# Layer 0's experts: rows fetched by a row list and answers scattered to a row per token and choice

## The chip, the cores and the metric

One core of a Trainium2 chip runs the whole program. The metric is the device time of one execution in microseconds (us), the median of several runs. The profile and the trace show one further execution.

The engines are named as in the profile: PE (TensorE matmuls) with PEld (its weight loads, which overlap the matmuls), DVE (VectorE), ACT (ScalarE), POOL (GpSimd) and SP (SyncE, which only issues transfers). Each runs its own list of instructions in order and waits on semaphores.

## The reference, cut to what matters

The model has four layers, each a cross attention and then a feed-forward part; 2 x 512 = 1024 tokens of 128 numbers. The change is in the feed-forward part of layer 0, whose end is a mixture of 16 experts with two choices per token. An expert takes at most 128 answers; of those that come in later, in token order, first choices first, none is computed:

```python
    B, S, D, H, E, F = (2, 128, 128, 16, 16, 512)     # B, S are taken from the input: 2 x 512
    xt = layer_norm(hidden, ln2_w, ln2_b).reshape(T, D)
    logits = xt @ router_w
    ...                                     # m1, m2: one-hot of the first and the second choice
    loc1 = jnp.cumsum(m1, axis=0) - 1.0
    loc2 = jnp.cumsum(m2, axis=0) - 1.0 + m1.sum(axis=0, keepdims=True)
    C = 2 * math.ceil(T / E)
    m1 = m1 * (loc1 < C)
    m2 = m2 * (loc2 < C)
    ...                                     # g1, g2: the two probabilities, normed to a sum of 1
    xin = jnp.einsum('tec,td->ecd', dispatch, xt)
    h = jnp.einsum('ecd,edf->ecf', xin, fc1_w) + fc1_b[:, None, :]
    h = jax.nn.gelu(h, approximate=False)
    eout = jnp.einsum('ecf,efd->ecd', h, fc2_w) + fc2_b[:, None, :]
    eout = eout * (1.0 - MOE_TOKEN_DROPOUT)
    moe_out = jnp.einsum('tec,ecd->td', combine, eout).reshape(b, s, D)
    return resid + moe_out
```

## The kernel before, in words

The four layers run one after the other. Tokens lie in SBUF as 8 tiles of 128 (`NT`); an expert's queue is one tile of 128 places. All arithmetic here is float32, in which each matmul shows as two rows of the trace.

**Places.** On DVE, `gating(0)` makes two one-hot masks (`top_mask`, L1786 to L1790; the last edit of the logits is L1808), the softmax (L1808 to L1812), and running sums of the masks (L1817 to L1820). PE turns these into the place of every token in its expert's queue (L2544 to L2546), which DVE masks with the capacity (L1823 to L1826).

**The experts' stage.** `run_queues` writes, for SP, PE, DVE and ACT, a loop over the 16 experts with steps that run ahead: DVE compares the places with 1 to 128 and gets a one-hot table of 1024 tokens x 128 places (`selected`, L2055, three experts ahead); PE gathers the expert's rows by 8 matmuls with that table (`queue`, L2694, two ahead); DVE applies the norm's weights (`features`, L2043); PE computes the hidden layer (L2703, one ahead), ACT the Gelu (L1299), PE the output (L2711), DVE copies it out (`answer`, L2049), and SP stores it to DRAM (`answers`, L678). Four buffers hold expert weights (`W0`); SP loads expert e+4 when expert e's output is done (`load_ahead`, L673). `gates0` (L1986 to L2004) works out the gates in the loop's first steps. PE turns the gates at the last step but two (`turned_gates`, L2632).

**After the experts.** PE computes the second biases (`biases`, L2640), which DVE adds (L1973); PE starts `prep(1)`, the next layer's cross attention's own keys and values (L2148 to L2195), whose values DVE copies out (`own_values`, L1463). DVE sums squares of layer 3's weights (L2071, eight of 1208 ns), which ACT squared before. POOL waits until every answer is stored, then gathers the answers back per token by 16 indirect transfers (`queues`, L916); DVE scales and adds each tile to the residual (L2080), and takes its moments (L1362). Then the next layer's norm begins (POOL L806, DVE L1388, PE L2216).

**Layers 1 and 3** already work as the change makes layer 0 work, with 15 and 23 tiles: `places` computes a list of DRAM rows per tile (L1901 to L1909 on DVE, L2566 on PE), POOL's `sorted_experts` fetches a tile's rows by it from `tokens_in` (L930) and scatters its answers by the same list to `sorted_out` (L935), PE turns the fetched tile (L2580) before the hidden layer (L2587) and the output (L2596), and SP brings the answers back (L769), which DVE adds (L1963). POOL first issues 8 fetches, then a scatter and a fetch in turn.

Of the kernel before, what the change touches and what calls it, by code (L numbers as in the profile page):

```python
# [59 lines left out]
SLOTS = E0 * CAPACITY  # L60
TOPK = {1: 1, 3: 2}
TILES = {l: TOPK[l] * B * S // P + 8 - 1 for l in TOPK}
# [6 lines left out]
def constants():  # L69
# [15 lines left out]
        "queue": np.broadcast_to(np.arange(E0, dtype=f) * CAPACITY - 1, (P, E0)),  # L85
# [104 lines left out]
def program(nc, x, mask, packed, experts, rows, zeros, out, answers, sorted_out, tokens_in, parts_q, parts_k, at):  # L190
# [3 lines left out]
    with ctx:  # L194
# [101 lines left out]
        D = take(dict(past_M=12032, w=2 * 1028, xin=4 * P, xe=2 * P, h=2 * 512, y=4 * P, back=16 * P, loc=256, slot=64))  # L296
        ranks, row_sums = D["xin"][:, 0:P], D["xin"][:, 2 * P:2 * P + 64]
        chosen = [D["back"][:, n * 1024:(n + 1) * 1024] for n in range(2)]
# [3 lines left out]
        R = {1: take(dict(past_Z=4096, back=NT * P, past_M=6912, xin=8 * P, xe=2 * P, h=2 * 512, y=4 * P, gap=608, w=8 * STRIDE[1])),  # L302
             3: take(dict(past_Z=1872, xe=2 * P, h=2 * 512, y=4 * P, xin=8 * P, back=2 * NT * P, diag=8 * P, gap=6640,
                          w=8 * STRIDE[3]))}
        assert all(sum(v.shape[-1] for v in r.values()) == ARENA for r in R.values())
# [39 lines left out]
        slots_ok, d_hot = sems("slots_ok d_hot")  # L345
# [31 lines left out]
        AFTER0, HELD0, STORED0, BACK0 = E0, 2 + E0, 16 * (1 + E0 // 4), 16 * 4  # L377
# [5 lines left out]
        def tiles_before(l):  # L383
            return E0 + sum(TILES[m] for m in SORTED if m < l)
# [7 lines left out]
        def weights_in(eng, l):  # L392
            for side in range(4):
                eng.wait_ge(w0_in[side], 16 * (E0 // 4 + 2 * (turn_of(l) + 1)))
# [200 lines left out]
        def run_queues(eng, *lagged):  # L595


            def steps(e, k, i):
                for do, ahead in lagged:
                    if isinstance(e, int) and not 0 <= e + ahead < E0:  # L600
                        continue
                    do(e + ahead, (k + ahead) % 4, i + (k + ahead) // 4)

            for e in range(-max(ahead for _, ahead in lagged), 0):
                steps(e, e, 0)
            with eng.Fori(0, E0 // 4 - 1) as i:
                for k in range(4):
                    steps(i * 4 + k, k, i)
            for k in range(4):
                steps(E0 - 4 + k, k, E0 // 4 - 1)  # L610

        def returns():

            return [(2 * b + k, k * NT + b * TB + t) for b in range(B) for k in range(2) for t in range(TB)]

# [39 lines left out]
        def _(sp):  # L655
# [19 lines left out]
            def store_answer(e, side):  # L675
                sp.wait_ge(d_y, e + 3)
                dst = answers.rearrange("(e p) d -> p e d", p=P)[:, bass.ds(e, 1), :]
                sp.dma_start(dst, D["y"][:, side * P:(side + 1) * P].unsqueeze(1)).then_inc(d_stored[side], 16)  # L678
# [65 lines left out]
            for l in SORTED:  # L744
                sp.dma_start(tokens_in[l][TOPK[l] * B * S:ROWS_OF[l], :], zeros[0:TILES[l] * P, :]).then_inc(cleared, 16)
            with sp.Fori(0, E0 // 4 - 1) as i:
                for k in range(4):
                    load_ahead(i * 4 + k, k)
                    store_answer(i * 4 + k, k)
            for k in range(4):  # L750
                store_answer(E0 - 4 + k, k)

            def sorted_experts(l):
# [5 lines left out]
                src = r_res if l == 1 else xn_moe  # L759
                sp.wait_ge(m_xn, B * (l + 1))  # L760
                for k in range(TOPK[l]):
                    sp.dma_start(tokens_in[l][k * B * S:(k + 1) * B * S, :].rearrange("(t p) d -> p t d", p=P),
                                 src[:, 0:NT * P].rearrange("p (t d) -> p t d", d=P)).then_inc(sent, 16)
                for side in range(4):
                    sp.wait_ge(d_back[side], BACK0 + 16 * side_total(l, side))
                for b in range(B):
                    for k in range(TOPK[l]):
                        first = k * B * S + b * S
                        sp.dma_start(R[l]["back"][:, first:first + S].rearrange("p (t d) -> p t d", d=P),  # L769
                                     sorted_out[l][first:first + S, :].rearrange("(t p) d -> p t d", p=P))\  # L770
                          .then_inc(d_stored[b * TOPK[l] + k], 16)

            sorted_experts(1)
# [20 lines left out]
        def _(pool):  # L794
# [115 lines left out]
            def queues():  # L910

                pool.wait_ge(slots_ok, 1)
                for side in range(4):
                    pool.wait_ge(d_stored[side], 16 * (1 + E0 // 4))
                for g, n in returns():
                    pool.indirect_dma_start(  # L916
                        D["back"][:, n * P:(n + 1) * P], None, answers,
                        bass.IndirectOffsetOnAxis(ap=slot_i[:, n:n + 1], axis=0))\
# [1856 lines left out]
```

## Time and profile before

| | |
|---|---|
| time, three runs | 1043.8, 1046.51, 1049.34 us; median 1046.51 |
| the profiled execution | 1044.33 us; span 1042.5 us, mean granted clock 0.868 |
| PE busy | 814.6 us (78%) |
| PEld busy | 568.4 us (55%) |
| DVE busy | 604.8 us (58%) |
| ACT busy | 395.0 us (38%) |
| POOL busy | 285.8 us (27%) |

The span is the profiled execution from its first to its last instruction; 1.8 us of its time lie around it. Busy shares are means over the whole program. The granted clock is PE's, as a share of its full rate (1.00 is 2.4 GHz, 0.50 is 1.2 GHz).

### The profile page before, as it was taken

Reading aid. Unit: us, or ns where it says so; the run is one execution under the profiler, and the core shown is the slowest. Engines: PE = TensorE matmul, PEld = TensorE weight load, DVE = VectorE, ACT = ScalarE, POOL = GpSimd, SP = SyncE. Lnnn points to the kernel's source line nnn. Section 1 sums busy time; section 2 is a strip of 40 time slices with the busy share of each in tenths; the row PEclk is TensorE's granted clock in tenths of the full one; section 3 lists DMA queues with packets and bytes.
Section 4 is the critical chain, followed back from the end, with each engine's and each line's share of the span. In section 5 each row is a group of like instructions: output and inputs, shape, how many; then the busy total and the mean of one; then the engine's idle time right before and its main releaser. Section 6 shows DMA issues by size and latency. Waiting matters only on the chain. (4 is left out here: it accounts for less than half of the span.)

```text
span 1042.5 us, 15008 instructions
## 1 busy us (share of the span) xinstructions
PE 814.6 (78%) x5075; PEld 568.4 (55%) x5075; DVE 604.8 (58%) x1317; ACT 395.0 (38%) x790; POOL 285.8 (27%) x310
## 2 busy tenths in 40 slices
PE   6896869966994764488778968999689998786794
PEld 4674434535994542487448832333246667574684
DVE  5884535626537656545757857777144454874542
ACT  2341435534332220044353414776532223342363
POOL 0443400100006320475464434101000001340574
PEclk9997879986996786588788976999989998997798
DMA  8005131042641400011000050410000100401113
GB/s 343 2 1 151 47 102 48 2 185 115 165 119 40 163 1 0 20 54 45 0 1 1 2 151 5 134 47 1 1 16 31 45 15 1 163 2 40 34 52 95
DMA packets 38980, 63.57 MB, mean 61 GB/s; under 512 B 4560, under 2 KB 30352, under 8 KB 38480
## 3 DMA queue, kind: packets, MB, share of 16 engines
q1 hardware_dynamic: 35968, 56.66, 16.9%
q0 software_dynamic: 2944, 6.04, 1.9%
q8 instruction: 39, 0.64, 0.3%
q14 instruction: 29, 0.24, 0.1%
HBM read 50.55 MB, written 14.42 MB: 62 GB/s over the span
## 5 line engine op out<-in xcount | busy, mean ns | idle before, releaser
L1625 DVE TENSOR_REDUCE arena<-psum 128x2 f32<-128x1024 f32 (+3 forms) x128 | 127.2, 1021 | 79.4 <-PE psum L2360 50.0
L1125 ACT ACTIVATE arena<-psum 128x512 f32<-128x512 f32 (+3 forms) x256 | 115.9, 516 | 86.6 <-PE psum L2373 48.7
L806 POOL TENSOR_TENSOR rstd<-var,held 128x8 f32<-128x8 f32 (+3 forms) x22 | 46.1, 2100 | 254.9 <-DVE var L1378 233.6
L2357 PE MATMUL psum<-arena 72*128 72x512 bf16 (+3 forms) x256 | 82.6, 394 | 24.7 <-DMA arena<-parts_q 11.7
L2285 PE MATMUL psum<-values_out_all,arena 128*128 128x128 f32 x560 | 77.8, 287 | 28.3 <-ACT arena L1089 28.2
L883 POOL TENSOR_TENSOR arena<-arena,small 128x616 f32<-128x616 f32 x56 | 67.9, 1215 | 111.6 <-DVE small L1557 111.3
L2285 PEld LDWEIGHTS psum<-values_out_all,arena 128*128 128x128 f32 x560 | 68.4, 195 | 38.1 <-ACT arena L1089 36.8
L2370 PE MATMUL psum<-arena 75*128 75x512 bf16 (+3 forms) x256 | 75.7, 361 | 9.8 <-DMA arena<-arena 8.0
L1076 ACT ACTIVATE arena<-arena 128x616 f32<-128x616 f32 x56 | 40.1, 717 | 109.5 <-DVE arena L1553 109.5
L1273 ACT ACTIVATE arena<-psum,arena 128x128 f32<-128x128 f32 x152 | 51.7, 421 | 53.1 <-PE psum L2587 53.1
L2357 PEld LDWEIGHTS psum<-arena 72*128 72x128 bf16 x256 | 23.4, 106 | 87.7 <-DVE arena L1625 45.9
L2661 PE MATMUL psum<-xT_all,wexp 128*128 128x512 f32 x144 | 67.0, 611 | 0.9 <-ACT arena L1226 0.6
L1549 DVE TENSOR_REDUCE small<-psum 128x8 f32<-128x616 f32 x56 | 44.0, 786 | 33.6 <-PE psum L2262 26.2
L2411 PE MATMUL psum<-arena 128*32 128x512 f32 (+3 forms) x512 | 60.3, 550 | 1.5 <-ACT arena L1138 1.5
L2262 PE MATMUL psum<-keys_of_tokens,xT_all 128*128 128x512 f32 (+1 forms) x160 | 52.9, 460 | 3.5 <-ACT xT_all L996 2.2
L896 POOL CAST arena<-arena 128x16 bf16<-128x16 f32 x16 | 3.4, 211 | 187.7 <-DVE arena L1625 187.7
L930 POOL DMA_INDIRECT arena<-tokens_in,row_i x38 | 37.1, 976 | 45.3 <-DVE row_i L1909 34.3
L1089 ACT ACTIVATE arena<-psum 128x640 f32<-128x640 f32 x56 | 38.7, 692 | 25.7 <-PE psum L2276 25.7
L2370 PEld LDWEIGHTS psum<-arena 75*128 75x128 bf16 x256 | 25.6, 103 | 41.8 <-ACT arena L1125 15.1
L2587 PE MATMUL psum<-arena,wexp 128*128 128x128 f32 x304 | 44.2, 292 | 2.7 <-DVE arena L1929 1.9
L1553 DVE TENSOR_TENSOR arena<-psum,small 128x616 f32<-128x616 f32 x56 | 44.8, 799 | 1.9
L1226 ACT ACTIVATE arena<-psum 128x512 f32<-128x512 f32 x36 | 21.4, 597 | 64.2 <-PE psum L2661 64.2
(331 smaller groups left out, 1663.4 us busy)
## 6 DMA issues: line engine op xcount, KB each, us to landing
arena<-experts SPq DMA_DIRECT2D x24, 514.0 KB, 6.2
parts_k<-wexp SPq DMA_DIRECT2D x12, 384.0 KB, 2.9
arena<-parts_k SPq DMA_DIRECT2D x48, 96.0 KB
arena<-parts_q SPq DMA_DIRECT2D x48, 96.0 KB
wexp<-experts SPq DMA_DIRECT2D x8, 514.0 KB, 3.7
arena<-rows SPq DMA_DIRECT2D x8, 512.0 KB, 8.0
wexp<-experts SPq DMA_DIRECT2D x9, 384.0 KB, 3.0
held<-packed SPq DMA_DIRECT2D x1, 2375.0 KB, 16.0
```

Of the source, the lines that this page charges most:

```text
L806: pool.tensor_tensor(dst, src, half[0:src.shape[0], 0:n], ALU.pow).then_inc(done, 1)
L883: pool.tensor_tensor(e, e, inv, ALU.mult).then_inc(e_mul, 1)
L1125: act.activation(p_self[:, n % 2, kt % 2, j, lo:S], bank(t_bank("keys", c, k), lo, S), ACT.Exp, scale=DS ** -0.5).then_inc(ut_ok, 1)
L1273: last = act.activation(r["h"][:, j % 2 * BANK + c * P:j % 2 * BANK + (c + 1) * P], bank(2 + j % 2, c * P, (c + 1) * P), func, **kw)
L1553: dve.tensor_tensor(weights_of(n), scores_of(n), wide_heads(part(n, 0)), ALU.subtract).then_inc(e_sub, 1)
L1625: dve.tensor_reduce(top[:, x % 2, qt, j:j + 2], src, AX_X, ALU.max, negate=True).then_inc(us_ok, 1)
L2262: last = mm(psum[:, first + lo:first + hi], tokens, rows[:, b, half, lo:hi], start=True, stop=True)
L2285: last = mm(bank(sum_bank(l, t), 0, P), PT3[l][:, n % 3, c * P:(c + 1) * P], VW[:, t // TB, half, c * P:(c + 1) * P], start=(half == 0 and ...
L2357: last = mm(bank(first + n, 0, W), q_ring[0:ROWS, x % 4, j + n, qt * P:(qt + 1) * P], k_ring[0:ROWS, x % 4, j + n, 0:W], start=True, stop= ...
L2370: last = mm(bank(first, lo, S), k_ring[0:ROWS + 3, x % 4, j, kt * P:(kt + 1) * P], q_ring[0:ROWS + 3, x % 4, j, lo:S], start=True, stop=True)
L2411: last = mm(psum[32 * j:32 * j + 32, 7 * BANK + lo:8 * BANK], v_wide[b][:, kt, 4 * g + j, :], p_self[:, n // 2 % 2, kt % 2, j, lo:S], star ...
L2661: mm(bank(c, 0, BANK), wexp[:, side, c * P:(c + 1) * P], xT_all[:, b * S:(b + 1) * S], start=True, stop=True).then_inc(h_ps, 1)
```

## The change

Layer 0 takes the scheme of layers 1 and 3. A list of 128 DRAM rows per expert (`row_i`) says where the row of each place in its queue lies in `tokens_in[0]`, which holds the normed tokens twice, once per choice, and 128 rows of zeros per expert behind them for places that no token fills. The answers are scattered by the same list to `sorted_out[0]`, which has one row per token and choice, so that four plain transfers bring them back.

- SP clears parts of four DRAM tensors right after its first loads, where it cleared two of them (2.4 MB) at 226 us; now 4.4 MB in all. It sends the tokens twice (2 x 512 KB) ahead of the experts' loop, and no longer stores answers in it. It waits for all scatters before the four transfers back.
- DVE: the new `places0` works out the row list; the softmax's sum, reciprocal and product move from the front into `gates0`, which now stands behind expert 1's answer, in 13 small instructions. The one-hot tables of each expert are gone. The eight sums of layer 3's squares move from behind the experts into steps 3 to 10, and the adding of the biases to step 11.
- PE: one transpose of the fetched tile takes the place of 8 gathering matmuls. Gates are turned behind expert 5, biases computed behind expert 9.
- POOL: 32 indirect transfers in the stage (16 fetches, 16 scatters) take the place of 16 behind it.
- ACT squares layer 3's weights ahead of the softmax's Exp, where that came first.

```diff
@@ sync
+            for l in SORTED:
+                sp.dma_start(tokens_in[l][TOPK[l] * B * S:ROWS_OF[l], :], zeros[0:TILES[l] * P, :]).then_inc(cleared, 16)
+            sp.dma_start(sorted_out[0][0:2 * B * S, :], zeros[0:2 * B * S, :]).then_inc(cleared, 16)
...
-            with sp.Fori(0, E0 // 4 - 1) as i:
-                for k in range(4):
-                    load_ahead(i * 4 + k, k)
-                    store_answer(i * 4 + k, k)
...
+            tokens_sent(0)
+            for e in range(E0 - 4):
+                load_ahead(e, e % 4)
+            answers_back(0)
@@ gpsimd
                 if l == 0:
-                    queues()
+                    sorted_experts(0)
@@ vector
+            def places0():
...
+                step.then(dve.scalar_tensor_tensor(M["mk"], bank(0, 0, 2 * n), float(CAPACITY), M["m12"], ALU.is_le, ALU.mult))
+
+                dve.tensor_tensor(which[:, :, 1, :], q3(M["mk"]), w("r_block").unsqueeze(2).broadcast_to(shape), ALU.mult)
+                dve.tensor_scalar(which[:, :, 0, :], q3(M["mk"]), w("r_lane"), None, ALU.mult)
+                step.then(dve.tensor_tensor(Z0["loc"], bank(0, 0, 2 * n), M["mk"], ALU.mult))
+                step.then(dve.tensor_reduce(lane, q3(Z0["loc"]), AX_X, ALU.add))
+                dve.tensor_tensor(lane_of0, lane.unsqueeze(2).broadcast_to([P, N, P]),
+                                  w("places").unsqueeze(1).broadcast_to([P, N, P]), ALU.is_equal).then_inc(g_m, 1)
+                dve.wait_ge(g_loc, 2)
...
+                dve.tensor_tensor(row_i[:, 0:E0], row, off, ALU.add).then_inc(slots_ok, 1)
...
+                features(0)
+                features(1)
+                for j in range(E0):
+                    if j + 2 < E0:
+                        features(j + 2)
+                    answer(j)
+                    if j == 1:
                         gates0()
-
-                run_queues(dve, (selected, 3), (weighed, 3), (features, 2), (answer, 0))
-                add_biases(0)
-                own_values(1)
...
+                    if 3 <= j < 11:
+                        last = row_sum(j - 3)
+                    if j == 11:
+                        add_biases(0)
...
+                own_values(1)
+                for b in range(B):
+                    for k in range(2):
+                        dve.wait_ge(d_stored[2 * b + k], 16)
...
@@ tensor
+                    pe.wait_ge(g_m, 2)
+                    for i in range(2 * NT):
+                        last = mm(bank(1, 0, 2 * E0), lane_of0[:, i, :], place_of0[:, i].rearrange("p k j -> p (k j)"),
+                                  start=(i == 0), stop=(i == 2 * NT - 1))
...
+                def turned(j):
+                    pe.wait_ge(q_in[j % 4], 16 * (j // 4 + 1))
+                    if j >= 2:
+                        pe.wait_ge(d_xe, j + 1)
+                    turn(bank(j % 2, 0, P), D["xin"][:, j % 8 * P:(j % 8 + 1) * P], ident).then_inc(d_T, 1)
...
+                pe.wait_ge(slots_ok, 1)
+                turned(0)
+                turned(1)
+                hidden(0)
+                for j in range(E0):
+                    if j + 2 < E0:
+                        turned(j + 2)
+                    if j + 1 < E0:
+                        hidden(j + 1)
+                    output(j)
+                    if j == 5:
                         turned_gates(0)
...
-                run_queues(pe, (gates_turned, 0), (queue, 2), (hidden, 1), (output, 0))
-                biases(0)
+                    if j == 9:
+                        biases(0)
+                pe.wait_ge(b2_ok, 1)
                 prep(1)
```

How the instructions stand on three engines, before and after. First PE, one expert in the middle of the stage, before: the gather of the expert after next (L2694), the hidden layer of the next (L2703), the output of this one (L2711).

```order
L2694 MATMUL psum<-arena,values_out_all 128x128 [waits d_xe,d_hot]
L2694 MATMUL psum<-arena,values_out_all 128x128 x7
L2703 MATMUL psum<-arena 128x128 [waits d_h,d_xe]
L2703 MATMUL psum<-arena 128x128 x3
L2711 MATMUL psum<-wexp,arena 128x128 [waits d_y,d_h]
L2711 MATMUL psum<-wexp,arena 128x128 x3
```

The same after: the transpose of the fetched rows (L2680), which waits for the fetch (`q_in`), then the hidden layer (L2688), which waits for the loaded weights (`w0_in`), and the output (L2697).

```order
L2680 MATMUL psum<-held,arena 128x128 [waits d_xe,q_in3]
L2688 MATMUL psum<-arena 128x128 [waits d_h,d_xe,w0_in2]
L2688 MATMUL psum<-arena 128x128 x3
L2697 MATMUL psum<-wexp,arena 128x128 [waits d_y,d_h]
L2697 MATMUL psum<-wexp,arena 128x128 x3
```

Eight matmuls gave way to one, and each transpose now waits for a transfer that POOL issued.

POOL from the norm ahead of the router (L806, `m_stat`) to the next layer's norm (L806, `x_stat`), before:

```order
L806 TENSOR_TENSOR rstd<-var,held 128x4 [waits m_stat]
L916 DMA arena<-answers,slot_i 128x128 [waits d_stored2,d_stored1,d_stored3,d_stored0,slots_ok]
L916 DMA arena<-answers,slot_i 128x128 x15
L806 TENSOR_TENSOR rstd<-var,held 128x8 [waits x_stat]
```

And after, the first rows of the stage's 32 transfers, of which the last eight are scatters:

```order
L900 DMA arena<-tokens_in,row_i 128x128 [waits slots_ok,sent,cleared]
L900 DMA arena<-tokens_in,row_i 128x128 x3
L900 DMA arena<-tokens_in,row_i 128x128 [waits q_in0]
L900 DMA arena<-tokens_in,row_i 128x128 [waits q_in1]
L900 DMA arena<-tokens_in,row_i 128x128 [waits q_in2]
L900 DMA arena<-tokens_in,row_i 128x128 [waits q_in3]
L905 DMA sorted_out<-arena,row_i 4096x128 [waits d_y]
L900 DMA arena<-tokens_in,row_i 128x128 [waits q_in0,d_T]
L905 DMA sorted_out<-arena,row_i 4096x128 [waits d_y]
```

The first transfer stood behind the last stored answer; now it stands behind the row list (`slots_ok`), the sent tokens and the cleared rows.

DVE from the last answers to the row sums, before:

```order
L2049 COPY arena<-psum 128x128 [waits d_stored3,d_O]
L1973 TENSOR_TENSOR x_res<-x_res,psum 128x1024 [waits gate_ok,b2_ps]
L1463 TENSOR_SCALAR arena<-psum,held 128x2x3x77 [waits v_ps,b2_ok]
L1463 TENSOR_SCALAR arena<-psum,held 128x2x3x77
L1463 TENSOR_SCALAR arena<-psum,held 128x2x77 x2
L2071 TENSOR_REDUCE arena<-arena 128x8 [waits n_sq] x8
```

After, two steps in the middle of the stage: the features of the tile after next (L2032), this tile's answer (L2039), one row sum (L2043).

```order
L2032 TENSOR_SCALAR arena<-psum,held 128x128 [waits d_T,d_H]
L2039 COPY arena<-psum 128x128 [waits d_back0,d_O]
L2043 TENSOR_REDUCE arena<-arena 128x8 [waits n_sq]
L2032 TENSOR_SCALAR arena<-psum,held 128x128 [waits d_T,d_H]
L2039 COPY arena<-psum 128x128 [waits d_back1,d_O]
L2043 TENSOR_REDUCE arena<-arena 128x8 [waits n_sq]
```

The row sums moved from behind the experts into their steps, and an answer now waits for the scatter that last read its buffer (`d_back`).

## Rows read from the trace of the kernel before

**Rows 1.** Windows: stretch, length, busy PE, PEld, DVE, ACT, POOL, granted clock, DMA share, GB/s.

```profile
258.50:310.20 51.70, 51.36 (x459) 50.90 (x457) 23.48 (x40) 19.33 (x62) 0.00 (x0) 1.00 0.52 142
310.20:337.00 26.80, 14.12 (x86) 13.09 (x86) 18.96 (x41) 5.89 (x11) 15.44 (x16) 0.73 0.16 42
```

**Rows 2.** Groups by line, 245 to 337 us: busy, mean ns, idle before.

```profile
L2694 PE MATMUL psum<-arena,values_out_all 128*128 128x128 f32 x256 | 34.0, 291 | 2.6 <-DVE arena L2055 2.6
L2071 DVE TENSOR_REDUCE arena<-arena 128x8 f32<-128x1024 f32 x8 | 9.1, 1208 | 0.0
L2080 DVE SCALAR_TENSOR_TENSOR x_res<-arena,x_res 128x128 f32<-128x128 f32 x16 | 4.5, 346 | 1.3 <-DMA arena<-answers,slot_i 1.3
```

**Rows 3.** Timeline of PE: start, duration, line, operation, in brackets the idle time before.

```profile
258.52 1.06 PE L2711 MATMUL psum<-wexp,arena 128*128 128x128 f32 x8
...
309.02 1.16 PE L2711 MATMUL psum<-arena 128*128 128x128 f32 x8 [0.34 <-ACT arena L1299]
310.11 2.05 PE L2640 MATMUL psum<-held,arena 16*128 16x128 f32 x16
313.47 2.42 PE L2148 MATMUL psum<-held 128*128 128x154 f32 x8 [1.31 <-DVE x_res L1973]
```

**Rows 4.** Timeline of POOL, the first and the last of 16 gathers.

```profile
313.01 1.20 POOL L916 DMA_INDIRECT arena<-answers,slot_i  x1 [82.24 <-DMA answers<-arena]
...
332.09 0.94 POOL L916 DMA_INDIRECT arena<-answers,slot_i  x1 [0.30 <-issue]
```

**Rows 5.** Timeline of DVE around the places and behind the experts.

```profile
239.84 0.29 DVE L1808 TENSOR_TENSOR arena<-arena,small 128x128 f32<-128x128 f32 x1
...
241.43 0.09 DVE L1817 MEMSET arena<- 128x32 f32 x1
...
245.90 0.42 DVE L1823 SCALAR_TENSOR_TENSOR arena<-psum,arena 128x256 f32<-128x256 f32 x1 [2.60 <-PE psum L2546]
...
318.06 1.88 DVE L1463 TENSOR_SCALAR arena<-psum,held 128x462 f32<-128x462 f32 x4 [4.64 <-PE psum L2152]
...
336.09 0.87 DVE L1362 BATCH_NORM_STATS2 stats<-x_res 128x6 f32<-128x128 f32 x4
```

**Rows 6.** Timeline of all engines, layer 3, from the one-hot table to the first tile.

```profile
967.25 2.29 DVE L1901 TENSOR_TENSOR arena<-arena,held 128x2048 bf16<-128x2048 f32 x1
...
970.45 0.18 DVE L1906 SCALAR_TENSOR_TENSOR arena<-psum,held 128x24 f32<-128x24 f32 x1 [0.92 <-PE psum L2566]
...
972.11 1.09 POOL L930 DMA_INDIRECT arena<-tokens_in,row_i  x1 [21.45 <-DVE row_i L1909]
...
974.73 0.48 PE L2580 MATMUL psum<-held,arena 128*128 128x128 f32 x1 [0.61 <-DMA arena<-tokens_in,row_i]
```

**Rows 7.** Timeline of PE, layer 3, the first tile's output.

```profile
979.97 1.85 PE L2596 MATMUL psum<-arena 128*128 x8
```

**Rows 8.** Timeline of PE, layer 1, the outputs of two tiles seven apart.

```profile
461.05 1.06 PE L2596 MATMUL psum<-arena 128*128 x8
...
474.82 1.06 PE L2596 MATMUL psum<-arena 128*128 x8
```

**Rows 9.** The loads of layer 0's expert weights (line L673), issue to landing.

```profile
DMA to landing us min/median/max: 3.5/3.7/8.1
```

**Rows 10.** Timeline, layer 3: the last of 23 scatters, the last add.

```profile
1030.57 0.97 POOL L935 DMA_INDIRECT sorted_out<-arena,row_i  x1 [0.37 <-DVE arena L1937]
...
1039.13 0.69 DVE L1963 TENSOR_TENSOR x_res<-x_res,arena 128x512 f32<-128x512 f32 x1 [0.17 <-DMA arena<-sorted_out]
```

**Rows 11.** Windows again, columns as in the first group: layer 2's start and layer 3's tiles.

```profile
490.00:495.00 5.00, 5.00 (x23) 5.00 (x23) 4.90 (x13) 1.41 (x2) 5.00 (x3) 0.50 0.02 3
985.00:1020.00 35.00, 33.55 (x271) 30.76 (x270) 16.16 (x48) 23.89 (x64) 26.95 (x27) 1.00 0.17 53
```

**Rows 12.** Timeline of PE, its pause ahead of layer 2's first low stretch.

```profile
488.72 1.61 PE L2187 MATMUL psum<-arena,held 128*128 128x154 f32 x10 [3.16 <-ACT arena L1012]
```

**Rows 13.** The page's DMA line, 40 slices of the span (26 us each), tenths busy.

```profile
DMA  8005131042641400011000050410000100401113
```

More of the change, by code:

```diff
@@ L187, in row_layout, with program @@
     return np.concatenate([w1.reshape(8, 4, P, P).transpose(0, 2, 1, 3).reshape(8, P, 4 * P), w2], 2)
-def program(nc, x, mask, packed, experts, rows, zeros, out, answers, sorted_out, tokens_in, parts_q, parts_k, at):
+def program(nc, x, mask, packed, experts, rows, zeros, out, sorted_out, tokens_in, parts_q, parts_k, at):
     ctx = ExitStack()
@@ L294, in program @@
         hT, sg, w2n = two(M["h"]), two(M["s"]), two(M["w2n"])
-        D = take(dict(past_M=12032, w=2 * 1028, xin=4 * P, xe=2 * P, h=2 * 512, y=4 * P, back=16 * P, loc=256, slot=64))
-        ranks, row_sums = D["xin"][:, 0:P], D["xin"][:, 2 * P:2 * P + 64]
-        chosen = [D["back"][:, n * 1024:(n + 1) * 1024] for n in range(2)]
+        D = take(dict(past_M=12032, w=2 * 1028, xin=8 * P, xe=2 * P, h=2 * 512, y=4 * P, back=16 * P, slot=64))
+        Z0 = take(dict(past_tokens=19936, lane=1024, which=256, loc=256, off=16, row=16))
         W0 = [wexp[:, 0, :], wexp[:, 1, :], D["w"][:, 0:1028], D["w"][:, 1028:2056]]
@@ L771, in sorted_experts @@
                           .then_inc(d_stored[b * TOPK[l] + k], 16)
+            def sorted_experts(l):
+                sp.wait_ge(x_xTp, B * (l + 1))
+                for e in range(8):
+                    first = e * STRIDE[l]
+                    sp.dma_start(R[l]["w"][:, first:first + 1028], experts[l][e]).then_inc(w0_in[e % 4], 16)
+                tokens_sent(l)
+                answers_back(l)
+            tokens_sent(0)
+            for e in range(E0 - 4):
+                load_ahead(e, e % 4)
+            answers_back(0)
             sorted_experts(1)
@@ L908, in selfattn @@
                 batch_tokens(1, m_stat, MOE_AT[l] + 2, m_rstd)
[L910 to L918, printed above, removed]
-                        .then_inc(d_back[g], 16)
             def sorted_experts(l):
@@ new lines, in gating @@
+                top_mask(t3(m1), LG, 0, shape)
+                step.then(dve.scalar_tensor_tensor(M["gc"][:, 0:n], m1, FMIN, logits[:, 0:n], ALU.mult, ALU.add))
+                top_mask(t3(m2), gc, 1, shape)
+                if l == 0:
+                    places0()
+                    return
+                dve.tensor_tensor(gc, LG, bc(small[:, 0, 0:NT]), ALU.subtract).then_inc(g_sub, 1)
+                dve.wait_ge(g_exp, [1, 0, 2][l])
+                step.then(dve.tensor_reduce(total, gc, AX_X, ALU.add))
@@ L1828, in gating @@
+                step.then(dve.reciprocal(total, total))
+                step.then(dve.tensor_tensor(gc, gc, bc(total), ALU.mult))
                 if l == 2:
@@ L2060, in weighed @@
[L2060 to L2071 removed]
+                raw = M["gb"][:, 0:64].rearrange("p (e c) -> p e c", c=8)
@@ L2770 @@
     parts_k = nc.dram_tensor("parts_k", (2, B, 3, 3 * P, S), BF16, kind="Internal").ap()
-    program(nc, ap["x"], ap["mask"], ap["packed"], [ap[f"experts{l}"] for l in range(4)], ap["rows"], ap["zeros"], out, answers,
+    program(nc, ap["x"], ap["mask"], ap["packed"], [ap[f"experts{l}"] for l in range(4)], ap["rows"], ap["zeros"], out,
             sorted_out, tokens_in, parts_q, parts_k, at)
```

250 lines of the change are left out of this document (101 added, 149 removed).

## The prediction

> **What bounds the kernel now.** I read the windows first. While the experts run, 258.5 to 310.2 us, PE is busy 51.4 of 51.7 us at a granted clock of 1.00, DVE 23.5, ACT 19.3, and POOL does nothing [rows 1]: the stage costs what PE issues. The groups by line say what that is: the gather by one-hot tables is 256 matmuls, 34.0 us of PE, two thirds of the stage [rows 2]. PE's timeline gives the period: the first output starts at 258.52, the last at 309.02 [rows 3], 50.5 us for 15 periods, 3.37 us each. Behind the stage the second window shows no engine full [rows 1], so there the waits count: POOL's first gather comes at 313.01 and its sixteenth at 332.09, 1.27 us apart [rows 4], and the last moments that the next layer needs end at 336.09 + 0.87 = 336.96 [rows 5]. From last output to that point is 27.9 us. Everything behind 336.96 is the next layer and is the same in both kernels, so I forecast when the moments end after the change, and shift the rest.
>
> **The front.** The second mask's last edit of logits starts at 239.84 and the running sums at 241.43 [rows 5]: the 1.6 us of softmax between them leave the path for `gates0`. The places then come back from PE at 245.90 - 1.6 = 244.3. New behind that are five instructions on tiles of 128 x 256 at 0.42 each [rows 5], with gaps 2.2, to 246.5; the one-hot table of 128 x 2048, which layer 3 makes in 2.29 us, then 16 small matmuls, 0.9 from its end to the next DVE step at 970.45, and 1.66 from there to the fetch (four small steps and POOL's start) [rows 6]. That puts the first fetch at 251.4. In layer 3 the fetched tile is turned 2.62 us after its fetch [rows 6], and the first output starts 5.24 us after that [rows 7]: 254.0 and 259.3. So the first output is 0.8 us later than now: the longer preparation costs what the missing gather and softmax give back.
>
> **The stage.** Per expert PE keeps one transpose, the hidden layer and the output. Layer 1 has that form at full clock: seven tiles in 474.82 - 461.05 = 13.77 us, 1.97 each [rows 8]. Fifteen periods are 29.5 us. To that I add:
> - 0.7, since layer 3's first output took 1.85 us where a warm one takes 1.06 [rows 7, 8].
> - 2.0 for `gates0` behind expert 1's answer: 13 small DVE instructions at about 0.29 [rows 5] are 3.8 us in which DVE hands PE nothing; PE has one period, about 1.8 to 2.0 us, in hand. Bounds 0 and 3.8.
> - 3.1 for the gates turned and the biases, which stand in the loop: 16 matmuls take 2.05 [rows 3], the 8 of the gates half of it.
> - 0.7 for eight row sums of 1.21 [rows 2]: with them a step has features 0.4, answer 0.3 and a sum, some 2.05 us with gaps, against PE's 1.97.
> - 1.5 for weights. A load starts when expert e's output is done and expert e+4 needs it: with PE three periods on, 3 x 1.97 = 5.9 us cover landing plus some 2.1 us of output, semaphore and issue. At the usual 3.7 us it just fits: 0. At 8.1, the longest seen [rows 9], a period becomes (8.1 + 2.1) / 3 = 3.4, and 12 loads cost 1.43 x 12 = 17.2, of which about 7 lie under the terms above: 10.2. I take a value near the median, since the longest was a load that shared the queues with other transfers.
> - 2.5 for the clock. After a pause of 3.16 us on PE [rows 12], 490 to 495 us went at 0.50 [rows 11]; five such microseconds cost 2.5. The pause of `gates0` is 2.0, between that and the pauses of under 1 us in layer 3's tiles, which kept 1.00 for 35 us [rows 11]. Bounds 0 and 5.
>
> Together 29.5 + 0.7 + 2.0 + 3.1 + 0.7 + 1.5 + 2.5 = 40.0 against 50.5. The last output starts at 299.3; its answer is copied by 300.8 (now 1.5 us after, too).
>
> POOL's 32 transfers need 31 x 1.27 us after the first: with first issue at 251.4 the last could go at 290.8, so 10 us of slack cover them; at 1.58 us per issue the cover is gone. Clearing 4.4 MB happens while the DMA engines idle: slices two and three (26 to 78 us) show 0 [rows 13], and the rows are wanted at 251. Sending the tokens costs nothing on the path either: SP issues it as soon as they are normed, before the router's logits, and the whole of the front up to the fetch at 251 is its cover.
>
> One rule speaks against this part. By the Trainium skill ("DMA: Bandwidth & Descriptors", section "Issuing engines are not separate DMA queues"), transfers started by different engines run on the same DMA engines and interleave. Here weight loads from SP and 32 row transfers from POOL would then share them; no stretch of this trace has both at once, so no row bears it out. By that rule the weights' term would be nearer its upper end, 10.2, and the time some 1030.
>
> **The tail.** PE goes from the last output straight to `prep(1)`: 1.1 us later, 300.4. From its start to the copy of its values takes 318.06 - 313.47 = 4.59 [rows 3, 5]: 305.0. The copies take 1.88 [rows 5], to 306.9, then come 16 adds of 4.5 in all [rows 2] and twice 0.87 of moments [rows 5], with gaps 6.5, to 313.4. Beside this run the answers: in layer 3 the last add starts 1039.13 - 1030.57 = 8.56 us after the last scatter [rows 10]. With a last scatter at 300.9 that is 309.5, and the last four adds are due at about 311, so it is covered by some 1.5 us; were it longer, the transfers back would set the end. The eight row sums, 9.1 us [rows 2], no longer stand between.
>
> **Sum.** 313.4 against 336.96: 23.6 us earlier, of which front and stage give 309.02 - 299.3 = 9.7 and the tail 27.94 - 14.1 = 13.8. The profiled execution took 1044.33 us, so 1020.7; the median of the three runs shown is 2.2 higher, so 1022.9. The next layer's PE pauses shrink as its `prep(1)` moves next to it, worth 0 to 2.5 at the price of low clock above; I take 0.9 of it: **1022.0**. If the gates' pause, the clock and the weights cost nothing, it is 6.0 less, and with the 2.5 in full another 1.6: 1014.4. If instead the weights come at 8.1 us and the clock loses the 5.0, it is 8.7 + 2.5 more: 1033.2.
>
> **Rivals.**
> (a) Weight loads bind: PE waits for each load, landing near 8 us. For it: the stage's DMA share is 0.52 already [rows 1], the same loads now come in fewer microseconds, with fetches and scatters among them. Against: median landing 3.7. Result 1022.0 + 8.7 = 1030.7. Chance 0.12.
> (b) Slower: the same mechanism, further out. If rows of 512 B delay each load so far that it lands after 13.5 us, twelve loads cost ((13.5 + 2.1) / 3 - 1.97) x 12 = 38.8, less 7 covered, 31.8 instead of 1.5: 1052.3. From about 12 us on the gain is gone. At twice the longest landing, 16.2, it is 1063. Against: nothing seen exceeds 8.1 [rows 9]. Chance 0.04.
> (c) PE's clock never comes up: each tile waits a little for its fetch, answer or weights. Then a period is twice 1.97, so 29.5 + 3.1 more, less about 6.4 of the terms above that such a slow PE covers: +26.2, 1048, no change. Against it: layer 3's tiles with the same waits hold 1.00 [rows 11]. Chance 0.06. The Trainium skill ("TensorE: Matmul & The Clock Gate", section "HAM oscillation — how this bites in real kernels") describes this case, where each burst of matmuls that follows a wait for a transfer starts cold; in layer 3's stretch the trace does not agree.
> (d) POOL binds: 32 issues at over 1.58 us each. The largest single one shown is 1.20 busy, 1.5 with its gap [rows 4]. At 2.0 the last scatter goes at 313.4, and the moments end 8.56 + 2.0 later, at 324.0: 1032.6. Chance 0.04.
>
> **How the numbers follow.** The forecast as summed has 0.74. A measurement of this kernel tells 0.5%, about 5 us, from no change. The forecast, (a) and (d) are faster: 0.90; (c) is the same: 0.06; (b) is slower: 0.04. The range of 1013 to 1034 holds the forecast with its bounds, and most of (a) and (d); what lies outside is (b), (c) and the far ends of (a) and (d), under 2 in 10.
>
> **What would show it.** In the profile of the changed kernel: first fetch near 251.4, first output near 259 and last near 299; a period of about 2 us with one pause after the third expert; clock 1.00 in most of the stage; loads landing in 4 to 5 us; the last scatter right behind the last answer; DVE's adds beginning near 307, moments done near 313. I am wrong on the weights if PE's idle time in the stage ends on transfers of expert weights; on the clock if long stretches show 0.50; on the tail if the adds wait for the answers back rather than DVE; on the front if the row list comes much after 250.

## The result

| | before | after |
|---|---|---|
| runs | 1043.1, 1043.8, 1046.51, 1049.34 us | 1011.85, 1014.13, 1015.86, 1016.39 us |
| median | 1045.15 us | 1015.0 us |
| the profiled execution | 1044.33 us | 1016.39 us |
| its span, granted clock | 1042.5 us, 0.868 | 1014.5 us, 0.872 |
| PE, DVE, POOL busy | 814.6, 604.8, 285.8 us | 788.4, 587.0, 301.8 us |

The ratio of the runs is 0.9716, with a 95% interval of 0.9685 to 0.9748: some 30 us faster. 1022.0 was forecast, with 1013 to 1034 as the range.

The windows of the kernel after, over its stage, its tail, the pause of `gates0` and the stretch behind that (stretch, length, busy PE, PEld, DVE, ACT, POOL, granted clock, DMA share, GB/s):

```profile
258.40:299.40 41.00, 35.39 (x278) 33.77 (x277) 22.33 (x50) 19.04 (x62) 24.10 (x25) 0.93 0.65 195
299.80:311.70 11.90, 9.22 (x70) 8.57 (x70) 8.33 (x31) 5.81 (x10) 0.97 (x1) 1.00 0.36 101
263.00:267.00 4.00, 1.36 (x13) 1.12 (x11) 3.59 (x14) 1.14 (x4) 2.12 (x3) 1.00 0.89 250
267.00:270.50 3.50, 3.44 (x17) 3.47 (x18) 0.48 (x2) 1.14 (x4) 1.95 (x2) 0.55 0.40 142
```

Against [rows 1]: PE fell from 51.4 to 35.4 us in the stage and has gaps now; the tail went from 26.8 us at a clock of 0.73 to 11.9 at 1.00.

PE's timeline in the kernel after: start, duration, and in brackets the idle time before.

```profile
258.36 1.92 PE L2697 MATMUL psum<-wexp,arena 128*128 128x128 f32 x8
...
261.30 1.06 PE L2697 MATMUL psum<-wexp,arena 128*128 128x128 f32 x8
...
263.19 1.06 PE L2697 MATMUL psum<-arena 128*128 128x128 f32 x8
264.09 0.27 PE L2680 MATMUL psum<-held,arena 128*128 128x128 f32 x1
267.06 1.78 PE L2688 MATMUL psum<-arena,wexp 128*128 128x128 f32 x8 [2.70 <-issue]
268.64 1.91 PE L2697 MATMUL psum<-arena 128*128 128x128 f32 x8
...
271.56 1.06 PE L2697 MATMUL psum<-wexp,arena 128*128 128x128 f32 x8
...
277.48 1.16 PE L2697 MATMUL psum<-arena 128*128 128x128 f32 x8 [1.10 <-ACT arena L1271]
...
295.79 1.16 PE L2688 MATMUL psum<-arena 128*128 128x128 f32 x8 [1.41 <-DMA arena<-experts]
...
298.22 1.16 PE L2697 MATMUL psum<-arena 128*128 128x128 f32 x8 [0.39 <-ACT arena L1271]
299.86 1.28 PE L2135 MATMUL psum<-held 128*128 128x154 f32 x8 [0.47 <-DVE arena L2039]
...
315.60 2.14 PE L2203 MATMUL psum<-held,arena 128*128 128x128 f32 x8 [5.38 <-DVE arena L1356]
```

The first output starts at 258.36 and the last at 298.22, where [rows 3] had 258.52 and 309.02: 39.9 us for 15 periods in place of 50.5. A plain period is 263.19 - 261.30 = 1.89 us where it was 3.37, some 22 us for fifteen; pauses, low clock, the gates and the biases take 11.4 of them back. No run puts the gathering matmuls back, so this part is a reading of the trace. Three waits stand out: 2.70 us ahead of expert 4's hidden layer, which ends when DVE, done with `gates0`, delivers the features (the row's "issue" is that wait); 1.10 for ACT, which copies the turned gates ahead of a Gelu; 1.41 for weights. A hidden layer takes 1.78 us right behind the pause and 1.16 later: the low clock in the fourth window. The last row, the next layer's transposes, is taken up below.

POOL's timeline behind the stage in the kernel after, its last scatter and the next layer's norm:

```profile
299.99 0.97 POOL L905 DMA_INDIRECT sorted_out<-arena,row_i  x1 [0.58 <-DVE arena L2039]
...
312.73 1.67 POOL L787 TENSOR_TENSOR rstd<-var,held 128x8 f32<-128x8 f32 x1 [11.77 <-DVE var L1346]
```

And DVE's, from the values' copy to the last moments:

```profile
302.23 1.88 DVE L1431 TENSOR_SCALAR arena<-psum,held 128x462 f32<-128x462 f32 x4 [2.13 <-PE psum L2139]
305.36 2.32 DVE L2068 SCALAR_TENSOR_TENSOR x_res<-arena,x_res 128x128 f32<-128x128 f32 x8 [1.26 <-DMA arena<-sorted_out]
...
310.83 0.87 DVE L1330 BATCH_NORM_STATS2 stats<-x_res 128x6 f32<-128x128 f32 x4
```

The moments end at 310.83 + 0.87 = 311.70, where [rows 5] had 336.96: 25.3 us of the gain stand there. DVE waits 1.26 us for the answers, so their way back ends last, by little.

In these two traces the next layer is 2.1 us shorter too. Its window from the norm behind the experts to the next norm, and the stretch in it from 356 to 364 us, in the kernel before:

```profile
338.00:382.50 44.50, 30.86 (x160) 22.73 (x160) 26.11 (x65) 12.10 (x18) 13.46 (x11) 0.81 0.25 96
...
356.00:364.00 8.00, 7.45 (x39) 6.05 (x39) 5.42 (x11) 2.90 (x5) 2.72 (x3) 0.79 0.00 2
```

And in the kernel after:

```profile
312.70:355.10 42.40, 28.33 (x160) 20.91 (x160) 25.95 (x65) 12.11 (x18) 13.47 (x11) 0.89 0.26 100
```

The same 160 PE instructions take 44.5 us at a clock of 0.81 and 42.4 at 0.89. Whether that is the change's doing is taken up below.

### The profile page after: what moved, and what is told of

It reads as the page before. It is cut to its first block and busy times, and to the rows that moved or that the text cites. A ratio compares the mean times of both kernels' runs of the same rounds, so it can differ in the third digit from the quotient of the medians.

```text
span 1014.5 us, 14411 instructions
## 1 busy us (share of the span) xinstructions
PE 788.4 (78%) x4846; PEld 540.6 (53%) x4851; DVE 587.0 (58%) x1304; ACT 394.6 (39%) x790; POOL 301.8 (30%) x326
## 5 line engine op out<-in xcount | busy, mean ns | idle before, releaser
L787 POOL TENSOR_TENSOR rstd<-var,held 128x8 f32<-128x8 f32 (+3 forms) x22 | 46.1, 2100 | 261.2 <-DVE var L1346 240.9
L2272 PE MATMUL psum<-values_out_all,arena 128*128 128x128 f32 x560 | 77.2, 286 | 28.2 <-ACT arena L1059 28.2
L900 POOL DMA_INDIRECT arena<-tokens_in,row_i x54 | 52.9, 980 | 70.1 <-DVE row_i L1896 34.3
L905 POOL DMA_INDIRECT sorted_out<-arena,row_i x54 | 53.4, 989 | 27.3 <-DVE arena L2039 12.9
```

The lines of the kernel that those rows point to most:

```text
L905: pool.indirect_dma_start(sorted_out[l], bass.IndirectOffsetOnAxis(ap=row_i[:, j:j + 1], axis=0), r["y"][:, j % 4 * P:(j % 4 + 1) * P], No ...
L2272: last = mm(bank(sum_bank(l, t), 0, P), PT3[l][:, n % 3, c * P:(c + 1) * P], VW[:, t // TB, half, c * P:(c + 1) * P], start=(half == 0 and ...
```

## The experiments

The theory: the stage is PE's own work, the pause of `gates0` with the low clock behind it, and small waits, with weight loads nearly hidden; the tail was POOL's gathers and is now the answers' way back, with DVE close to it; the rest is PE's clock behind shorter idle times. The rivals are that weight loads bind the stage, that DVE's sums were the tail, and that the last part is not the clock.

Single executions scatter by some 5 us ahead of the change, so the traces are compared by stretches. "Experts" is from first to last output, "layer 0" from POOL's norm ahead of the router to the one behind the experts, "next" from there to the following norm (starts of POOL's rows, L787 after, L806 before). The ratio is to the kernel before on the same chip; the medians come from several chips, so kernels are compared by the ratio.

| run | ratio, 95% interval | median us | experts | layer 0 | next |
|---|---|---|---|---|---|
| before | 1 | 1045.15 | 50.5 | 108.2 | 44.5 |
| after | 0.9716 [0.9685, 0.9748] | 1015.0 | 39.9 | 83.6 | 42.4 |
| after, again | 0.9722 [0.9695, 0.9749] | 1014.58 | 37.4 | 80.4 | 42.5 |
| gates spread | 0.9720 [0.9667, 0.9773] | 1012.5 | 35.9 | 79.0 | 42.9 |
| weights once | 0.9715 [0.9651, 0.9779] | 1013.78 | 38.2 | 81.5 | 42.9 |
| loads doubled | 0.9815 [0.9761, 0.9870] | 1023.84 | 46.8 | 90.3 | 42.4 |
| gathered back | 0.9898 [0.9843, 0.9952] | 1030.72 | 38.8 | 97.3 | 42.3 |
| sums behind | 0.9797 [0.9777, 0.9817] | 1022.15 | 36.2 | 87.6 | 43.9 |
| PE filled | 0.9729 [0.9698, 0.9761] | 1015.2 | 36.7 | 80.4 | 41.9 |
| both cures | 0.9673 [0.9640, 0.9705] | 1009.57 | 35.3 | 77.9 | 40.7 |
| before, sums ahead | 1.0029 [1.0004, 1.0054] | 1046.14 | 50.5 | 109.8 | 42.9 |
| before, PE filled | 0.9961 [0.9938, 0.9983] | 1039.65 | 50.5 | 108.7 | 40.7 |

**The way back, undone.** The 16 gathers of before, over the changed kernel's rows.

```diff
-            answers_back(0)
...
+                            pool.indirect_dma_start(D["back"][:, n * P:(n + 1) * P], None, sorted_out[0][0:2 * B * S, :],
+                                                    bass.IndirectOffsetOnAxis(ap=slot_i[:, n:n + 1], axis=0))\
+                                .then_inc(q_in[2 * b + k], 16)
...
```

> The changed kernel with the answers brought back as before: 16 indirect gathers on POOL behind the last scatter's landing, in place of SP's four transfers (two small DVE instructions more, for the list of rows). Theory (the tail ends on the answers' way back): gathers start about 2.4 us after the last scatter's issue, 302.4, the sixteenth 19.1 us later, landing 2.5 us on, last adds done near 325.5 instead of 311.7: 13 to 14 us slower, 1028.5 us. Rival (what the tail gained is PE's and DVE's earlier work, and the way back is hidden): under 3 us slower.

POOL's timeline: the last scatter, the first and the last gather.

```profile
298.10 0.97 POOL L904 DMA_INDIRECT sorted_out<-arena,row_i  x1 [0.58 <-DVE arena L2051]
301.13 0.99 POOL L925 DMA_INDIRECT arena<-sorted_out,slot_i  x1 [2.07 <-DMA sorted_out<-arena,row_i]
...
319.92 0.94 POOL L925 DMA_INDIRECT arena<-sorted_out,slot_i  x1 [0.30 <-issue]
```

From the first gather's start to the last's it is 18.8 us, and layer 0 is 13.7 us longer than in the trace of after, as the theory said. By the ratios it is 1.8%, some 19 us, and their intervals together leave room for 12 to 26. DVE idles four times ahead of its adds, 15.8 us in all, and from the last output to the moments it takes 28.2 us, as much as before the change (27.9), although the sums are out of the way. It costs more than the sums do, the other part of the change that a run puts back.

**Sums ahead, in the kernel before.** The other half of the old tail, moved alone.

```diff
-                run_queues(dve, (selected, 3), (weighed, 3), (features, 2), (answer, 0))
+                run_queues(dve, (selected, 3), (weighed, 3), (features, 2), (answer, 0), (summed, 0))
...
```

> The kernel before with one part of the change alone: the eight row sums of layer 3's squares, 9.1 us of DVE behind the experts, move into the last four steps of the experts' loop, two in each. Theory (before, POOL's 16 gathers ended the tail; the sums lay beside them): the moments end where they did, 27.9 us behind the last output, within 0.5 us; the last four steps of the loop grow by 0 to 2 us, as DVE then has 4.0 us of work in a step of 3.57; time 0 to 2 us longer. Rival (DVE's sums stood between the experts and the next layer): up to 9 us faster.

DVE's timeline, the four groups of adds; then POOL's first gather, and PE's transposes of the next layer:

```profile
321.77 1.13 DVE L2088 SCALAR_TENSOR_TENSOR x_res<-arena,x_res 128x128 f32<-128x128 f32 x4
326.09 1.14 DVE L2088 SCALAR_TENSOR_TENSOR x_res<-arena,x_res 128x128 f32<-128x128 f32 x4 [3.18 <-DMA arena<-answers,slot_i]
...
330.95 1.15 DVE L2088 SCALAR_TENSOR_TENSOR x_res<-arena,x_res 128x128 f32<-128x128 f32 x4 [2.82 <-DMA arena<-answers,slot_i]
336.32 1.14 DVE L2088 SCALAR_TENSOR_TENSOR x_res<-arena,x_res 128x128 f32<-128x128 f32 x4 [4.21 <-DMA arena<-answers,slot_i]
...
314.43 1.20 POOL L916 DMA_INDIRECT arena<-answers,slot_i  x1 [83.79 <-DMA answers<-arena]
...
342.27 2.14 PE L2224 MATMUL psum<-held,arena 128*128 128x128 f32 x8 [14.78 <-DVE arena L1388]
```

Where the sums stood, DVE now waits 10.2 us for gathers. The rival, that DVE's sums alone were the tail, falls. The moments end 29.6 us behind the last output, not at the 27.9 expected, and the price lay elsewhere than expected: not in the stage (50.5 us still) but behind it, as the last answer's copy now stands behind sums, so gathers began 5.6 us after the last output (4.0 in [rows 3, 4]).

**Sums behind, in the kernel after.**

```diff
-                    if 3 <= j < 11:
-                        last = row_sum(j - 3)
...
+                own_values(1)
+                for e in range(8):
+                    last = row_sum(e)
...
-                own_values(1)
```

> The changed kernel with the eight row sums put back behind the experts, behind own_values. Theory: 9.1 us of sums on DVE, which idles 1.3 us there for the answers, so the moments end 8 us later; in the stage nothing is won, since PE never waited for a sum there: 8 us slower, 1023 us. Rival (the sums lengthen the stage as the prediction's 0.7 us says, or more): less than 7.5 us slower, with a stage that is 0.7 us or more shorter.

PE's last output, and DVE's sums and last moments:

```profile
297.25 1.16 PE L2697 MATMUL psum<-arena 128*128 128x128 f32 x8 [0.39 <-ACT arena L1271]
...
303.05 9.09 DVE L2043 TENSOR_REDUCE arena<-arena 128x8 f32<-128x1024 f32 x8
...
318.02 0.87 DVE L1330 BATCH_NORM_STATS2 stats<-x_res 128x6 f32<-128x128 f32 x4
```

From the last output to the moments it takes 21.6 us in place of 13.5, and the ratio goes from 0.9716 to 0.9797. So the two halves of the tail are worth their full price only together. With gathers the tail is 27.9 us with the sums behind, and without them 29.6 in the kernel before and 28.2 in the changed one: moving the sums alone gains nothing. With plain transfers it is 21.6 and 13.5. The 6.3 us from 27.9 to 21.6 are not the transfers' alone, since DVE's copy of the values also starts 5.0 us sooner after the last output (4.0 us, 9.0 in [rows 3, 5]). The stage is 3.6 us shorter than in the first trace of after, but by 1.1 us than in the second, and the wait for weights (0.27 instead of 1.31) accounts for nearly all of that. The sums cost the stage nothing that shows.

**Weights left out, and doubled.**

```diff
...
-            for e in range(E0 - 4):
-                load_ahead(e, e % 4)
...
```

> The changed kernel without the 12 loads of weights in the stage: experts 4 to 15 use the weights of experts 0 to 3, so the answers of twelve experts are others. Theory (weights are nearly hidden: one wait of 1.4 us in the trace): 1.4 to 2 us faster, 1013 us; scatters may land sooner than their 3.9 us, which gives nothing, since the last one's landing alone counts. Rival (loads bind, or slow fetches and scatters): 5 us or more faster.

```diff
                 sp.wait_ge(d_O, e + 1)
+                sp.dma_start(more[e * 1028:(e + 1) * 1028, :], zeros[0:1028, :]).then_inc(more_in, 16)
                 load0(e + 4, side)
...
```

> The changed kernel with as many bytes again ahead of each of the 12 weight loads: 514 KB of zeros from DRAM to a DRAM tensor that nobody reads. Theory: a load's landing grows from 4.6 us to between 6 and 9; by the sum of the prediction, at 8.1 us the loads cost 10.2 us instead of 1.4 to 1.5, so 4 to 10 us slower, 1019 to 1025 us, with PE's idle time ending on transfers of weights. Rival (the loads are far from binding): under 1.5 us slower.

Without the loads, layer 0 is 2.1 us shorter than in the first trace of after, which has the same low clock, and 1.1 longer than in the second, which has not; the ratio is the same within its interval. Row transfers land sooner without the loads. The issues of scatters from 254 to 300 us (count, median landing), in the kernel after and without the loads:

```profile
sorted_out<-arena,row_i POOLq DMA_INDIRECT x16, 3.9
...
sorted_out<-arena,row_i POOLq DMA_INDIRECT x16, 2.3
```

The loads' line in the kernel after:

```profile
DMA to landing us min/median/max: 3.4/4.6/6.6
```

The same with doubled bytes:

```profile
DMA to landing us min/median/max: 3.4/6.4/8.9
```

And there PE's waits for weights from 254 to 312 us (total, times, longest):

```profile
PE psum L2691 <- DMA arena<-experts: 4.6, 5, 1.6
PE psum L2691 <- DMA wexp<-experts: 3.4, 4, 1.6
```

Nine waits of 8.0 us in all, layer 0 6.8 us longer than in the first trace of after: with a median landing of 4.6 the loads are on the edge, and two microseconds more bring a wait to nine of the twelve hidden layers that use loaded weights. Rival (a) of the prediction is right as a mechanism and was not reached.

**The gates spread.**

```diff
...
-                    if j == 1:
-                        gates0()
...
+                    if 1 <= j < 5:
+                        gates0(j - 1)
...
```

> The changed kernel with gates0 cut into four pieces of 3 to 4 small instructions, one behind each of the answers of experts 1 to 4; row sums move two steps on, the adding of the biases too. Theory (the pause of gates0 and the low clock behind it cost 2.7 + 1.7 us of the stage): PE's pause ahead of expert 4's hidden layer goes, the granted clock stays at 1.00 from about 260 us on, and the last output comes 3 to 4.4 us earlier; time 1011 us. Rival (the weight loads set the stage's length, and the pause only hides part of a wait for them): the idle time moves to the loads, and the time stays within 1 us of the changed kernel's 1015.

PE's timeline, in the places where it waits:

```profile
263.76 1.16 PE L2690 MATMUL psum<-arena,wexp 128*128 128x128 f32 x8 [0.82 <-DMA wexp<-experts]
...
266.30 1.16 PE L2690 MATMUL psum<-arena 128*128 128x128 f32 x8 [0.38 <-DMA arena<-experts]
...
289.26 1.16 PE L2690 MATMUL psum<-arena 128*128 128x128 f32 x8 [0.83 <-DMA arena<-experts]
```

The pause is gone and the clock holds, but waits for weights grew from 1.4 to 2.0 us. Against the first trace of after the stage is 4.0 us shorter, against the second 1.5, and the ratio is that of the change alone. The times show no gain.

**The change again.**

> The changed kernel itself once more, on the same chip as the run with both cures, to set that beside it. 1012 to 1017 us. In its trace the pause of gates0 is 2.7 us again; whether the clock falls behind it is open: it fell in the trace of the changed kernel, and not in the one with the row sums put back, with the same pause.

Its PE, at the first output and at the same pause:

```profile
258.65 1.06 PE L2697 MATMUL psum<-wexp,arena 128*128 128x128 f32 x8
...
263.34 0.27 PE L2680 MATMUL psum<-held,arena 128*128 128x128 f32 x1
266.29 1.13 PE L2688 MATMUL psum<-arena,wexp 128*128 128x128 f32 x8 [2.68 <-issue]
267.26 1.06 PE L2697 MATMUL psum<-arena 128*128 128x128 f32 x8
```

A pause of 2.68 us, and the hidden layer behind it takes 1.13 us, not 1.78: no low clock. It also came up earlier here, so that the first output took 1.06 us, not 1.92. The same instructions thus differ by 2.5 us in the stage, and from the norm ahead of the router to the one behind the experts the change gains 24.7 us in the first trace and 27.8 in this one. With a pause of 2.7 us the clock fell in four traces (after, weights once, loads doubled, gathered back) and not in two (this one, sums behind). The four are those whose first output still ran at half clock (1.91 to 1.92 us); in the two it took 1.06 and 1.16. Why the clock comes up sooner in some executions, and whether that decides what the pause does, is not shown.

**PE filled, in the kernel before.**

```diff
                 biases(0)
+                filled(5, 2)
                 prep(1)
+                filled(60, 6)
```

`filled(n, at)` issues n matmuls of ones into bank `at`, which is free there.

> The kernel before with 65 matmuls of 128 x 128 on PE that nobody reads, 5 behind the biases and 60 behind prep(1), so that PE hardly idles from the last output to the next layer's transposes. Theory (PE's low clock behind that idle time costs the next layer 2 to 3 us, which the changed kernel wins back): the granted clock stays at 1.00 from 313 to 341 us, values are copied 2.2 us sooner, which changes nothing for the gathers; from the moments on the next layer is 2 to 4 us shorter; time 1041 to 1043 us where before is 1045. Rival (those 2.1 us come from something other than the clock): within 1 us of before at that place.

The window over the next layer, as above:

```profile
339.80:380.60 40.80, 28.42 (x184) 21.93 (x182) 25.90 (x65) 12.11 (x18) 13.52 (x12) 0.98 0.28 104
```

At a clock of 0.98 the next layer takes 40.7 us where it took 44.5, and matmuls that nobody reads make the kernel before 0.4% faster. Ahead of that the clock was still 0.57 at 313 to 318 us, as the five matmuls came behind a wait of 1.31 us; there the theory's 1.00 was not met. That the clock costs the next layer some 2 to 4 us is so. But that the change wins part of it back is not shown: the run with sums ahead, a kernel before with 14.78 us of idle PE at that place, has this window:

```profile
339.40:382.20 42.80, 28.63 (x160) 21.16 (x160) 25.98 (x65) 12.11 (x18) 13.47 (x11) 0.86 0.26 99
```

That is 42.8 us without the change's shorter idle time, within the 42.3 to 43.9 of the unfilled changed kernels. Both kinds start the layer at half clock (8 transposes in 2.14 us, behind a pause of 14.78 as behind one of 5.38), and the 44.5 of the first trace had one more stretch of low clock, 356 to 364 us at 0.79. The part of the theory that gave the change a share of the next layer's clock falls.

**PE filled, and both cures, in the kernel after.** `filled(n)` is the same for bank 6.

```diff
+                    filled(9)
                     pe.wait_ge(g_m, 2)
...
+                filled(10)
                 pe.wait_ge(slots_ok, 1)
...
+                    if j == 3:
+                        filled(9)
...
                 prep(1)
+                filled(20)
```

> The changed kernel with matmuls of 128 x 128 that nobody reads in four idle places of PE: 9 and 10 while the row list and the first fetch are made, 9 ahead of expert 4's hidden layer, 20 behind prep(1). Theory (the clock costs about 2 us at the stage's start, 1.7 behind the pause of gates0 and 2 to 3 in the next layer's start): the clock is 1.00 from the first output on, without the dip at 267 us; the first output comes 1.5 to 3 us earlier after the first fetch, the stage is 1.7 to 2.5 us shorter, the next layer 2 to 4 us shorter: 1007 to 1010 us. Rival (a pause does not set the clock, or filling delays the work behind it): no change or slower.

This missed. The fillings were too short: PE still idled 2.25 us ahead of the first tile, and the first hidden layers ran low again (1.92 and 1.44 us); 1.46 us of idle stayed behind prep(1), and the clock fell to 0.72 at 316 to 322 us. Longer ones (9 and 18 ahead of the first tile, 25 behind prep(1)), with the gates spread and so none at the pause:

> The changed kernel with both cures: gates0 in four pieces as in the run with spread gates, and matmuls that nobody reads on PE, 9 and 18 ahead of the first tile and 25 behind prep(1). Theory: the two gains add up, as they lie at different places: 4.0 us of the stage from the spread gates, 0.6 to 1.6 us before the first output and 2 to 3 us in the next layer's start from the clock: 6.5 to 8.5 us faster than the changed kernel, some 1007 us on a chip where that takes 1015. Rival (idle time moves: with a faster PE the weight loads end last): the waits for weights grow from 1.4 to 2 us to over 4, and the gain stays under 5 us.

Its windows up to the first output, over the experts, and over the next layer:

```profile
254.00:260.10 6.10, 4.78 (x38) 4.07 (x36) 1.23 (x3) 1.14 (x4) 4.65 (x5) 1.00 0.14 43
260.10:295.50 35.40, 31.96 (x271) 30.34 (x270) 22.23 (x50) 17.97 (x62) 24.31 (x25) 1.00 0.75 228
...
309.30:350.00 40.70, 29.50 (x194) 23.02 (x192) 25.78 (x66) 12.12 (x18) 13.47 (x11) 0.99 0.28 104
```

The clock is 1.00 or 0.99 throughout. Layer 0 and the next are together 7.3 us shorter than in the first trace of after and 4.2 than in the second; the median is 5.0 us under the change's on the same chip (1009.57 and 1014.58), less than the 6.5 to 8.5 expected, and the intervals of the two ratios overlap by a little. The waits for weights are 2.0 us, as with the gates spread alone, so that rival is not what is missing; the first trace of after, from which the gains were taken, was one of low clock. Both cures together give the lowest ratio of the kernels run.

## Why the prediction was right, and where its sizes were off

- **Bound and front.** As said: first fetch at 250.4 (251.4 forecast), first output 258.4 (259.3); 0.6 us of that difference stands at the router's norm already, ahead of the places.
- **The stage.** 39.9 us against 40.0, but with other parts: that the sum met this trace is luck, and the second trace of the same kernel has 37.4. A plain period is 1.9 us, not 1.97, which is 1 us for fifteen. `gates0`: the outputs at 263.19, 268.64 and 271.56 are 5.45 and 2.92 us apart where 1.9 is usual, 4.6 us more, of which 2.7 are the pause; the sum had 4.5; but the low clock is there in one trace and missing in the next, so the clock's term of 2.5 is a chance, as its bounds of 0 to 5 had it. Gates turned and biases: the 3.1 us of PE's work and a wait of 1.10 behind it, as ACT's copy of the turned gates stands ahead of a Gelu that PE needs; the sum left that out. Weights: 1.4 against 1.5. Row sums: nothing against 0.7. The Trainium skill's rule that transfers of several issuers interleave ("DMA: Bandwidth & Descriptors", section "Issuing engines are not separate DMA queues") agrees with the runs in its direction: loads from SP land after a median of 4.6 us, 3.7 in [rows 9], and POOL's scatters after 3.9 beside the loads and 2.3 without them. The upper end for which the prediction used it, 10.2 us, was far too much here: the waits for weights are 1.4.
- **The tail.** 13.5 us against 14.1. The term that was mis-sized is `prep(1)` to its values, 4.59 us in the sum: the row it came from ran at a clock of 0.50, and right behind the experts it takes 302.23 - 299.86 = 2.4. DVE was therefore ready early, and the "cover" of 1.5 us over the answers' way back turned into a wait of 1.26 for it (0.98 in the second trace). By the prediction's own sign, adds that wait for the answers rather than for DVE, the chain that ended last was the other one.
- **The next layer.** 0.9 us was taken for "PE pauses shrink". The two traces differ by 2.1, but the kernel before with sums ahead takes 42.8 us without the shorter pauses, so the step is not borne out: behind a pause of 5.4 us, where the run with sums ahead has 14.8, the layer's transposes still start at half clock.
- **The rest of the distance to 1015.0.** Against the profiled execution the forecast was 1.7 us short up to the moments and 1.2 in the next layer, and 0.6 more come behind. The other 3.6 are the step from profiled execution to median, which was taken as +2.2 from before; after, the profiled execution is the slowest of four, 1.4 above the median. That is scatter and no mechanism. The low end of the range stood for a stage without pause, low clock and waits; the measured time came near it in other ways.
- **Rivals.** (b) and (d) did not come: no load landed later than 6.6 us, and POOL idled 0.58 us ahead of its last scatter, waiting for the last answer. (c) did not come either: the clock is 0.93 over the whole stage. Work that starts at half clock behind a wait was seen at the first tiles, behind the wait for the first fetch, and at the pause of `gates0`, there in some executions alone.

## What to carry to other kernels

Where two chains end together, as POOL's gathers and DVE's sums did here, moving one can gain nothing, as the sums' did, and its full worth shows only when the other is gone; a test of the sums alone would have spoken against moving them. When a duration is carried from one place to another, look up the granted clock of the row it comes from. And a block of small instructions in a pipelined loop becomes a pause by as much as it exceeds the work that the next engine has in hand, here about one period; cut into pieces it left no pause in the trace, though the times show no gain from that alone.

## What was not expected

The same pause of 2.7 us lowered PE's clock in four of six traces, with nearly the same instructions around it; one trace says little about a clock at such a place. Matmuls without use, put where PE idled, made the kernel before 3.5 us faster (1039.65 against 1043.14 on that chip), which was expected; not expected was that the layer behind them, 40.7 us there, differs between kernels without them by as much as 44.5 and 42.8 at nearly the same idle time.
